# Relation layers of a graph network: rolled loops with a picked index column and fp32 rows, against one straight block with fp16 high/low rows

## What is computed

```
seg = tgt * R + edge_type                      # R = 16 relations
msg = x[src]                                   # a row of 128 per edge
agg = segment_sum(msg, seg).reshape(N, R, d)
cnt = segment_sum(ones, seg).reshape(N, R, 1)
agg = agg / clip(cnt, 1)                       # mean per node and relation
out = einsum('nrd,rdo->no', agg, W_r) + x @ root_r + bias_r
x = relu(out)                                  # not after layer 3
```

## Time and profile before

| | us |
|---|---|
| median of three runs | 5518.86 |
| the three runs | 5373.97, 5518.86, 5620.42 |
| span of the profiled execution | 5583.3 |
| busy in it: PE, PEld, DVE, ACT, POOL | 3604, 2657, 1899, 1308, 2433 |

### The profile page before, as it was taken

One profiled execution on the slowest core, in us unless ns is written; L12 is line 12 of the kernel. 1 busy time (PEld: TensorE's weight loads), 2 busy tenths in 40 slices (PEclk: granted clock), 3 DMA queues, 4 the chain that ended last, 5 costly groups with the idle time before them and its releaser, 6 DMA issues. The chain is left out here.

```text
span 5583.3 us, 78623 instructions
## 1 busy us (share of the span) xinstructions
PE 3604.0 (65%) x16642; PEld 2657.4 (48%) x16643; DVE 1899.3 (34%) x5702; ACT 1308.1 (23%) x4264; POOL 2432.6 (44%) x2452
## 2 busy tenths in 40 slices
PE   1625567898577777776667765565567656556556
PEld 1424444555355555555455554444445544444444
DVE  6467765442222222222222221221232222122122
ACT  2249951111121111111121111111111111111111
POOL 0010000000366666666566665545546655554554
PEclk9998888999777778777787776666677766666666
DMA  0010001101211111111211111111121111111111
GB/s 16 0 38 0 0 20 52 47 19 53 67 43 43 43 44 43 43 43 44 53 42 43 44 40 35 36 33 36 36 64 43 43 37 34 35 35 34 36 35 40
DMA packets 128987, 208.51 MB, mean 37 GB/s; under 512 B 41426, under 2 KB 82748, under 8 KB 128940
## 3 DMA queue, kind: packets, MB, share of 16 engines
q0 software_dynamic: 80304, 169.17, 11.7%
q1 hardware_dynamic: 48636, 38.79, 2.4%
HBM read 186.12 MB, written 21.68 MB: 37 GB/s over the span
## 5 line engine op out<-in xcount | busy, mean ns | idle before, releaser
L1311 POOL DMA_INDIRECT arena<-rows,arena x2424 | 2380.5, 982 | 1738.3 <-ACT arena L1325 1023.3
L1446 PE MATMUL psum<-arena 128*128 128x80 f32 (+1 forms) x4896 | 1017.1, 403 | 1198.4 <-ACT arena L1332 794.1
L1441 PE MATMUL psum<-arena 128*128 128x320 f32 x4848 | 1650.5, 499 | 198.1 <-DVE arena L1375 117.8
L1446 PEld LDWEIGHTS psum<-arena 128*128 128x128 f32 x4896 | 986.1, 312 | 1275.4 <-issue 1272.0
L1441 PEld LDWEIGHTS psum<-arena 128*128 128x128 f32 x4848 | 1063.2, 225 | 726.4 <-issue 278.7
L1325 ACT ACTIVATE arena<-arena 128x1 int32 (+1 forms) x2424 | 483.4, 202 | 3281.7 <-PE psum L1441 1820.6
L1385 DVE TENSOR_TENSOR arena<-arena,psum 128x20 f32 x606 | 106.6, 176 | 2924.7 <-PE psum L1446 1557.0
L1375 DVE TENSOR_SCALAR arena<-arena 128x320 f32<-128x320 f32 x2424 | 893.5, 445 | 47.2 <-DVE arena L1385 31.1
L1044 PE MATMUL psum<-arena,h 128*128 x1750 | 488.8, 384 | 38.8 <-DMA h<-h 38.8
L913 POOL DMA_DIRECT2D h<-h x16 | 13.9, 873 | 933.4 <-issue 435.5
L1046 PE MATMUL psum<-arena,h 128*128 x1750 | 386.4, 221 | 0.0
(11 more groups left out here) (150 smaller groups left out, 1562.0 us busy)
## 6 DMA issues: line engine op xcount, KB each, us to landing
arena<-rows,arena POOLq DMA_INDIRECT x2424
h<-work SPq DMA_DIRECT2D x15, 640.0 KB, 3.4
h<-h POOLq DMA_DIRECT2D x15, 640.0 KB, 6.4
rows<-arena SPq DMA_DIRECT2D x12, 256.0 KB
x_pad<-arena SPq DMA_DIRECT2D x1, 1600.0 KB, 7.3
h<-arena SPq DMA_DIRECT2D x1, 1600.0 KB, 12.4
work<-x_pad SPq DMA_DIRECT2D x5, 320.0 KB, 3.2
x<-work SPq DMA_DIRECT2D x5, 320.0 KB, 2.5
```

The costliest lines, as they stand in the source:

```text
L1311: e.indirect_dma_start(out=t.msg[:, k, :], out_offset=None, in_=d[f"rows_{l}"][:, :], in_offset=bass.IndirectOffsetOnAxis(ap=t.pick[:, k:k ...
L1441: e.matmul(p.psum[:, MEAN + g, 0:REL * WIN], t.msg[:, k, :], t.oh[:, k, :], start=(k % GT == 0), stop=(k % GT == GT - 1)).then_inc(s_ag, 1)
L1446: m = e.matmul(p.psum[:, OUT, 0:groups * WIN], t.wr[:, r, :], t.agg[:, r, 0:groups, :].rearrange("p g w -> p (g w)"), start=(r == 0), stop ...
```

## The change

The three relation layers and their setup become one block, `relations`, written out straight (no loops). In it:

- POOL gathers straight with a column of the index table `idx`, with no copy to `pick`, from a table `pair_l` that holds each row as two fp16 halves (high and low, 2 x 128 values, 512 bytes as before). It runs up to ROWS_AHEAD = 12 groups (48 tiles) ahead of the matmuls, and waits once per group.
- DVE makes one-hots in fp16 with values 0 and 1, from an fp16 iota, up to HOTS = 4 groups ahead.
- PE multiplies high and low halves by the same fp16 one-hot, eight matmuls of 320 columns per group.
- The mean is a table `winv` of 1/count per window, broadcast by SP for eight groups at a time; DVE multiplies by it when it takes the sums out of PSUM. It takes over what ACT did there.
- The 16 weights are applied to eight groups at once (160 columns).
- At a layer's end ACT scales to the high half and DVE makes the low half; a bound on the values gives the scale, from sums of |W| on PE.
- `edge_weights` is replaced by `window_weights`: DVE takes max and reciprocal of the counts, and DVE and ACT copy 202 windows of 20 columns; the last GCN layer also writes `pair_0` (two DVE operations and a store per group of 640 nodes, five groups).

One-hots come four at a time with a mean and an add between them, where a round had sixteen in one or two bursts. The diff, cut to its core:

```diff
-        def gather(i, k):
-            held(e, s_pk, i * PER + k + 1, passed)
-            e.indirect_dma_start(out=t.msg[:, k, :], out_offset=None, in_=d[f"rows_{l}"][:, :],
-                                 in_offset=bass.IndirectOffsetOnAxis(ap=t.pick[:, k:k + 1], axis=0)
-                                 ).then_inc(s_got[k], 16)
...
+            for g in range(NG):
+                at = l * NG + g
+                if at >= ROWS_AHEAD:
+                    e.wait_ge(s_mm, at - ROWS_AHEAD + 1)
+                for k in range(GT):
+                    tile = g * GT + k
+                    e.indirect_dma_start(
+                        out=t.msg[:, at % ROWS_AHEAD, k].rearrange("p h f -> p (h f)"), out_offset=None,
+                        in_=d[f"pair_{l}"].rearrange("n h f -> n (h f)"),
+                        in_offset=bass.IndirectOffsetOnAxis(ap=t.idx[:, tile:tile + 1], axis=0)
+                    ).then_inc(s_got[at % ROWS_AHEAD], 16)
...
+                e.wait_ge(s_oh, GT * (at + 1))
+                if at >= 4:
+                    e.wait_ge(s_ev, at - 3)
+                for k in range(GT):
+                    for half in range(2):
+                        m = e.matmul(p.psum[:, at % 4, 0:KEYS], t.msg[:, at % ROWS_AHEAD, k, half, :],
+                                     t.oh[:, at % HOTS, k, :], start=(k == 0 and half == 0),
+                                     stop=(k == GT - 1 and half == 1))
+                m.then_inc(s_mm, 1)
+                if g and g % BATCH == 0:
+                    apply(g // BATCH - 1)
...
-                e.tensor_scalar(t.oh[:, k, :], t.iota, t.stage[:, k:k + 1], t.stage[:, PER + k:PER + k + 1],
-                                ALU.is_equal, ALU.mult).then_inc(s_oh, 1)
+                e.tensor_scalar(t.oh[:, at % HOTS, k, :], t.iota, t.key[:, tile:tile + 1], None,
+                                ALU.is_equal).then_inc(s_oh, 1)
...
+            e.scalar_tensor_tensor(t.agg[batch % 2][:, :, k, :],
+                                   p.psum[:, at % 4, 0:KEYS].rearrange("p (r w) -> p r w", r=REL),
+                                   t.back[:, l:l + 1], t.winv[batch % 2][:, k, :].rearrange("p (r w) -> p r w", r=REL),
+                                   ALU.mult, ALU.mult).then_inc(s_ev, 1)
...
+    def copies(e, regs, first, copy):
+        for g0 in range(first, NG, 2 * LOAD):
+            n = min(LOAD, NG - g0)
+            e.load(regs[0:n], t.gbase[0:1, g0:g0 + n])
+            for k in range(n):
+                base = e.snap(regs[k], min_val=0, max_val=NODES - 1)
+                copy(t.windows[:, g0 + k, :], t.inverse[:, bass.ds(base, WIN)]).then_inc(s_win, 1)
...
+        e.scalar_tensor_tensor(t.wgt, t.typf, float(WIN), t.dloc, ALU.mult, ALU.add).then_inc(s_key, 1)
+        v.link(e, e.tensor_scalar(t.inverse, t.cnt[0:REL, :], 1.0, None, ALU.max))
+        e.reciprocal(t.inverse, t.inverse).then_inc(s_inv, 1)
...
+            if batch >= 2:
+                e.wait_ge(s_ev, groups_before(batch - 1))
+            e.dma_start(t.winv[batch % 2][:, 0:n, :], d["winv"][g0:g0 + n].rearrange("g r w -> g (r w)")
+                        .partition_broadcast(P)).then_inc(s_wi[batch % 2], 16)
...
             if last:
                 e.sem_inc(s_vq)
                 v.link(e, e.tensor_scalar(ex, ex, 0.0, None, ALU.max))
+                v.link(e, e.tensor_scalar(pair[:, :, 0, :], ex, PAIR_SCALE0, None, ALU.mult))
+                v.link(e, e.scalar_tensor_tensor(pair[:, :, 1, :], ex, PAIR_SCALE0, pair[:, :, 0, :], ALU.mult, ALU.subtract))
                 e.sem_inc(s_vq)
```

More of the change, by code:

```diff
@@ L545, in _ @@
-        with e.Fori(0, ROUNDS // 2) as i:
-            v.enter(i, 4)
-            for par in range(2):
-                select(i * 2 + par, par)
-                e.wait_ge(s_oh, v.now())
-            v.leave(ROUNDS // 2)
-        select(ROUNDS - 1, 0)
-        e.wait_ge(s_oh, v.now())
-        finish_weights(e, v, p, t, s_dg, s_sq)
+        v = Tally(s_seen)
+        regs = [e.alloc_register(f"win_v{k}") for k in range(LOAD)]
+        e.scalar_tensor_tensor(t.wgt, t.typf, float(WIN), t.dloc, ALU.mult, ALU.add).then_inc(s_key, 1)
@@ L568, in _ @@
-        with e.Fori(0, ROUNDS // 2) as i:
-            for par in range(2):
-                take(i * 2 + par, par)
-        take(ROUNDS - 1, 0)
+        regs = [e.alloc_register(f"win_a{k}") for k in range(LOAD)]
+        e.wait_ge(s_inv, 1)
+        copies(e, regs, LOAD, lambda out, at: e.activation(out, at, ACT.Copy))
         root_of_degree(e, t, s_dg, s_sq)
@@ L1174, in relation_memory, with relations_general, body @@
     return t
+def relations_general(p, t):
+    parts, done = [], None
+    for stage in range(4):
+        part, done = relation_setup(p, t) if stage == 0 else relation_layer_general(p, t, stage - 1, done)
+        parts.append(part)
+    block = Bodies()
+    for name in parts[0].of:
+        def body(e, name=name):
+            for part in parts:
+                part.of[name](e)
+        block.of[name] = body
+    return block
 def relation_setup(p, t):
-    nc, d = p.nc, p.d
-    s_ld, s_io, s_tr, s_ev, s_r = p.sem("loaded"), p.sem("iota"), p.sem("transposed"), p.sem("evacuated"), p.sem("rows")
+    d = p.d
+    s_ld, s_io, s_tr, s_ev, s_r, s_done = (p.sem(n) for n in (
+        "loaded", "iota", "transposed", "evacuated", "rows", "set_up"))
     block = Bodies()
@@ L1254, in general_relations, with relation_layer_general @@
     return Serial(p, steps, EDGE_TILES)
-def relation_layer(p, t, l, fast):
-    nc, d = p.nc, p.d
-    PER = ROUND
-    G = PER // GT
-    FULL = EDGE_TILES // PER
-    REST = EDGE_TILES - FULL * PER
-    last = l == 2
-    s_ld, s_x1, s_rt, s_ac, s_pk, s_oh, s_ag, s_ev, s_ot, s_ad, s_fr = (p.sem(n) for n in (
-        "weights", "x1", "root", "root_added", "picked", "onehots", "means", "evacuated", "outputs", "added", "freed"))
-    s_hr, s_so = p.sem("by_nodes"), p.sem("stored")
-    s_got = [p.sem(f"rows{k}") for k in range(PER)]
-    passed = p.sem("passed")
-    loop = None
-    if not fast:
-        loop, s_go = general_relations(p, t, l), p.sem("constants")
-    MEAN, OUT = 0, 4
+def relation_layer_general(p, t, l, before):
+    d = p.d
+    last = l == 2
+    s_ld, s_x1, s_rt, s_ac, s_fr, s_hr, s_so, s_done = (p.sem(n) for n in (
+        "weights", "x1", "root", "root_added", "freed", "by_nodes", "stored", "layer_done"))
+    loop = general_relations(p, t, l)
     block = Bodies()
@@ L1461, in _, with batch_size, groups_before, pair_memory @@
                 m.then_inc(s_fr, 1)
+    return block, s_done
+NG = EDGE_TILES // GT
+KEYS = REL * WIN
+BATCH = 8
+NB = -(-NG // BATCH)
+ROWS_AHEAD = 12
+HOTS = 4
+CHUNKS = [(c, 4 * c, min(BLOCKS, 4 * c + 4)) for c in range(7)]
+TURN_BANK = (0, 1, 2, 3, 6)
+def batch_size(b):
+    return min(BATCH, NG - b * BATCH)
+def groups_before(batch):
+    return batch // NB * NG + batch % NB * BATCH
+def pair_memory(p):
+    t = Bag()
+    c = p.carve(0)
+    rows = c(NPAD)
+    t.hrows = rows.rearrange("p (b f) -> p b f", b=BLOCKS)
+    t.pairs = rows.bitcast(F16).rearrange("p (b h f) -> p b h f", b=BLOCKS, h=2)
+    t.ht, t.acc = c(NPAD), c(NPAD)
+    t.x1 = c(NPAD).rearrange("p (b f) -> p b f", b=BLOCKS)
+    t.wr = [c(REL * RF).rearrange("p (r o) -> p r o", r=REL) for _ in range(2)]
+    t.root = [c(RF) for _ in range(2)]
+    t.bias = [c(1) for _ in range(2)]
+    t.absw = c((REL + 1) * RF + 1)
+    t.idx, t.key = c(EDGE_TILES, I32), c(EDGE_TILES)
+    t.gbase = c(GPAD, I32)
+    t.iota = c(KEYS // 2, F16)
+    t.oh = c(HOTS * GT * KEYS // 2, F16).rearrange("p (s k n) -> p s k n", s=HOTS, k=GT)
+    t.agg = [c(KEYS * BATCH).rearrange("p (r g w) -> p r g w", r=REL, g=BATCH) for _ in range(2)]
+    t.ones = c(P)
+    t.bound, t.tops, t.scale, t.back = c(3), c(2), c(3), c(3)
+    t.msg = p.h16[:, :, :, :].rearrange("p a b c -> p (a b c)")[:, 0:ROWS_AHEAD * GT * 2 * RF].rearrange(
+        "p (s k h f) -> p s k h f", s=ROWS_AHEAD, k=GT, h=2)
+    t.winv = [p.work[:, q * KEYS * BATCH:(q + 1) * KEYS * BATCH].rearrange("p (g n) -> p g n", g=BATCH) for q in range(2)]
+    return t
```

498 lines of the change are left out of this document (283 added, 215 removed).

## The result

The changed kernel takes 4951.01 us (median of four, 4944.83 to 4952.52); the kernel before took 5515.73 on the same chip (median of four, 5373.97 to 5620.42). The changed kernel's time is 1091 us over the predicted 3860, outside the range of 3780 to 4380. The profiled execution has a span of 4948.1 us.

What follows compares the result with a forecast made beforehand. POOL's gathers were taken to bound the changed kernel, with no gap between them: 1405 until the first gather + 2380 gathers + 48 borders + 24 tail = 3857, say 3860 us; range 3780 to 4380.

Steps and rivals of the forecast that it cites:

- a cycle of waits: Old relation layers: no engine full; ACT waits 1821 us for PE, POOL idles 1738 us before gathers, sixteen buffers the only slack.
- PE's clock would go with the rounds: Relation layers: what PE's clock made of the old rounds should vanish with them; time between layers equal whatever the granted clock.
- POOL's gap: Idle time between POOL's gathers, 0.30 us each, 2098 times, 715 us in all before; set at zero in the forecast.
- so I take the gap to be that of the increment and register work: POOL's 0.30 us before gathers: ascribed to `held` (wait, increment) and set at zero; otherwise 727 us stay.
- the gap is the gather's own: Rival on POOL's gathers: 0.30 us stay ahead of each, 3860 + 727 = 4590 us; chance 0.12.
- PE is just under POOL even in the worst clock: PE in the relation layers: 3.2 to 4.1 us per group at the lower clock level, against POOL's 3.93.
- a sign that PE or DVE is the bound: Sign that the forecast is wrong, in the relation layers: POOL waiting for sums of PE.
- The lock: DVE one-hots and POOL gathers exclude each other; rival with each burst paid in full: 4420 us, chance 0.06.
- The 0.982 already holds it: POOL's gathers: the mean of 0.982 us already includes DVE's interference, 92 us over 2424 gathers before.
- Until the first gather: Setup before the relation layers: 1441 - 44 + 3 + 5 = 1405 us, with `edge_weights` replaced at 87 to 90 against 133.
- Borders and tail: Two borders between relation layers at 24 us each (20 to 35), 48 together; 24 us after the last gather.
- Broadcasts, adds, one-hots, mean: Relation layers: broadcasts 10 us each, hidden; one-hots under 1.1 us per group, mean 0.49, add under 0.5; DVE no bound.

## Why the prediction was wrong

**What bounds the kernel.** Right for the kernel before as far as it went (a cycle of waits), wrong in what bounds each engine inside it: I read 1.25 us per gather as 0.94 of work and a removable 0.30. Right as well, as far as the profiles reach, was that PE's clock would go with the rounds as a cause of differences. From the first gather of a layer to its last the kernel before took 1235, 1373 and 1432 us at clocks of 0.76, 0.72 and 0.69, the changed one 1152, 1149 and 1151 at 0.67, 0.66 and 0.65. The last three clocks lie close together, so this is a sign and no proof.

**POOL's gap, the main miss: 702 of 1091 us.** The step "so I take the gap to be that of the increment and register work" failed. The earlier trace rows compared gathers with direct transfers, and the run with plain copies shows that this was the difference. Both bounds were named, 0 and 727; I chose the wrong one, and gave the rival "the gap is the gather's own" 0.12. What should have weighed more is how even the gap was: 2123 of the 2423 gaps between the gathers of the kernel before are 0.30 or 0.31 us (the earlier trace rows sums them with a few others), the sign of a fixed price. That rival's time, 4590, still lies 361 us short of the measured one, because of the stalls.

**The stalls, 434 us.** No rival had them. "PE is just under POOL even in the worst clock" is right by its work: the run with one long one-hot instruction shows PE waiting for gathers with the full eight matmuls. What the sum put at nothing without a reason is a wait of POOL for sums that PE's records show as long finished: its term for PE was work alone. The prediction named such a wait as a sign that PE or DVE is the bound; by their work neither is. Beside back-to-back gathers the records of another engine can come only every 0.70 us, and PE's sums are seen late even where the records show no such steps. Both were gone with copies. They struck PE or DVE (1295 us on DVE where PE had little to do). The stalls stayed at 341 to 571 us whatever was changed in the columns of the work, the form of PE's code, bytes, rows, broadcasts or slack, and were absent where DVE had one one-hot instruction. What causes them stays open, and so does why they are absent there. DVE had fewer instructions, but gathers also came more slowly, 1.44 instead of 1.25 us apart, and no run separated the two. Open is also what the 0.70 us are: every execution here is recorded by the profiler, and I cannot exclude that the recording of instructions takes part.

**The lock.** "The 0.982 already holds it" was right for the changed kernel (0.956; gathers beside one-hots 0.977, others 0.946). The Trainium skill's "SBUF — State Buffer", section "Who interferes with whom", has such an exclusion for two kinds of DVE instruction: those in a two-port mode, where the later one is blocked for the whole instruction, and those with two inputs in SBUF, against a GpSimd instruction that reads SBUF. The long pass is of the second kind, and a gather reads its index column there; its 1.435 and 1.829 us agree. The four short fp16 passes are of an operation that it counts to the first kind, and the trace shows next to nothing of that lock: 0.03 us a gather.

**Until the first gather.** Predicted 44 us saved in `edge_weights`, measured 76 (POOL's first clearing of the adjacency begins at 207.81 instead of 283.55). The reciprocal took 20.1 us as predicted; 13 blocks of window copies, on DVE and ACT side by side (73 and 80 instructions between 160 and 190, first row of the stretches above), went by in 23 us, 1.8 a block instead of 3.3. For overhead and store, put at 18 us, some 9 are left. The last GCN layer and the setup took the rest back: 1380.5 against 1405.

**Borders and tail.** 38.3 us between the last gather of layer one and the first of layer two, predicted 24:

```profile
2531.46 0.94 POOL L1406 DMA_INDIRECT h<-pair,arena  x1 [0.30 <-issue]
2570.66 0.94 POOL L1406 DMA_INDIRECT h<-pair,arena  x1 [38.26 <-DMA pair<-arena]
```

POOL ends while PE still has up to 12 groups to go: after 4911.9 PE runs nine groups of sums before the last weights, 36 us of tail instead of 24. Slack that hides a stall inside a layer is paid back at its end. With six groups ahead (`ROWS_AHEAD = 6`) the borders were 59 us together instead of 79, and the tail 24 instead of 36.

**Broadcasts, adds, one-hots, mean:** as predicted (one-hots 309 ns, mean 547, add 165; the broadcast landed in 6 us).

## What to carry to other kernels

A small idle time that is equal at thousands of instances of one instruction is that instruction's price until an experiment shows otherwise; plain copies in place of the gathers would have told in one run. When an engine's gap is called "issue", look at whether instructions come at an even step: here cutting columns, bytes or slack was then of no use, and only other instructions beside the gathers ended the stalls. And when one loss vanishes, take the sum of all three terms (work, gaps, stalls) before calling it a gain: one long pass removed 434 us of stalls and added 432 us of work.

## What the runs showed of the hardware

- An indirect gather of 128 rows on POOL costs 1.25 us (0.944 and a gap of 0.305); with half the bytes 1.25, with 64 rows 1.21 (0.907 and the same gap). A plain copy of the same 64 KB: 0.54.
- Beside such gathers PE or DVE can fall into steps of 0.70 us (817 on PE in the changed kernel, 848 us in all), and PE's sums are used 9.1 us (at a layer's start up to 63 us) after the record of their last matmul. With plain copies, which come more than twice as fast, the steps are gone and the sums are used after 1.4 us.
- One-hot passes of 1280 columns from two repeated inputs take 1.48 us each, and a gather that meets one grows from 0.944 to 1.435 or 1.829 us; four passes of 320 columns that compare with one key per partition take about 1.0 together, and a gather beside them 0.977.
- The kernel before ran 4653 us on one chip and 5983 on another, at mean granted clocks of 0.89 and 0.74. Over the five chips of the experiments the time goes with the clock; that the clock alone makes the difference is not shown.
